# Two accumulator banks for probabilities times values, and a ring of two banks for the other steps

## The reference

```
x = LN(x + attention0(x))      # 16 query heads on 4 key/value heads, RMS norm, rotary, full softmax
x = LN(x + experts(x))         # top 1 of 8 experts, gate/up/down of width 512, and a shared expert of the same width
x = LN(x + attention1(x))      # 16 heads of 16, biases, causal softmax
x = LN(x + mlp(x))             # 256 -> 1024 -> 256, relu, 4 bit weights with scales, low-rank additions
attention:  probs = softmax(q k^T / 4);  out = (probs v) Wo
```

## Time and profile before

| | |
|---|---|
| median of 3 runs | 843.1 us (842.71 to 844.33) |
| the profiled execution's own time | 843.22 us |
| its span in the profile | 841.4 us |
| TensorE busy | 773.6 us (92%) |
| VectorE busy | 449.0 us (53%) |
| ScalarE busy | 357.3 us (42%) |
| mean granted TensorE clock | 0.982 |
| first layer's attention | 35 to 248 us |
| tiles of the experts | 286 to 422 us |
| second layer's attention | 498 to 788 us |

### The profile page before, as it was taken

The page is one execution under the profiler, slowest core; times in us unless marked ns, Lnnn a source line. Parts: engine busy times, 40 slices in busy tenths (PEclk is TensorE's granted clock), DMA queues, the critical chain, the costliest instruction groups (busy, mean ns, idle before and its releaser), DMA issues. The chain is left out here.

```text
span 841.4 us, 11574 instructions
## 1 busy us (share of the span) xinstructions
PE 773.6 (92%) x3933; PEld 410.9 (49%) x3934; DVE 449.0 (53%) x1202; ACT 357.3 (42%) x561; POOL 115.7 (14%) x127
## 2 busy tenths in 40 slices
PE   7899999999999999999997979888998999889886
PEld 3323435444335466666664444344464445433675
DVE  4662852563446522222266767868655775672453
ACT  3498785784872112212134233445413532246030
POOL 0000000000000311112851501131001100022000
PEclk9999999999999999999999999989999999999999
DMA  6767026006026251111137850017200460000000
GB/s 220 202 212 263 1 80 183 1 30 184 0 79 222 66 165 48 44 44 44 32 91 226 239 149 1 1 35 234 60 1 2 133 194 1 2 1 26 14 13 25
DMA packets 52029, 75.01 MB, mean 89 GB/s; under 512 B 7670, under 2 KB 44826, under 8 KB 50058
## 3 DMA queue, kind: packets, MB, share of 16 engines
q1 hardware_dynamic: 50108, 69.26, 27.2%
q0 software_dynamic: 1872, 5.11, 2.3%
HBM read 46.57 MB, written 27.66 MB: 88 GB/s over the span
## 5 line engine op out<-in xcount | busy, mean ns | idle before, releaser
L659 PE MATMUL ps<-arena 128*128 128x256 f32 (+3 forms) x1084 | 323.1, 446 | 18.1 <-ACT arena L1066 3.0
L659 PEld LDWEIGHTS ps<-arena 128*128 128x128 f32 x1084 | 199.0, 193 | 104.7 <-issue 66.2
L992 ACT ACTIVATE arena<-ps 128x1024 f32<-128x1024 f32 x128 | 124.0, 1030 | 26.2 <-PE ps L727 25.7
L1089 ACT ACTIVATE arena<-ps 128x1024 f32<-128x1024 f32 (+3 forms) x128 | 82.9, 702 | 114.3 <-PE ps L919 114.2
L1475 DVE TENSOR_REDUCE arena<-ps 128x1 f32<-128x512 f32 (+3 forms) x176 | 100.5, 634 | 27.6 <-PE ps L897 26.7
L785 PE MATMUL ps<-arena 128*128 x184 | 86.5, 593 | 0.6 <-DVE arena L1199 0.6
L1590 POOL TENSOR_SCALAR_AFFINE_SELECT arena<-arena 128x512 f32<-128x512 f32 x64 | 41.9, 655 | 254.1 <-ACT arena L1089 254.1
L727 PE MATMUL ps<-arena 96*128 96x512 bf16 x256 | 69.8, 382 | 4.4 <-ACT arena L992 3.0
L895 PE MATMUL ps<-arena 96*128 96x128 bf16 (+3 forms) x256 | 62.6, 304 | 9.6 <-DVE arena L1475 5.4
L741 PE MATMUL ps<-arena 128*32 128x512 f32 x512 | 68.8, 604 | 0.2 <-ACT arena L999 0.2
L1020 ACT ACTIVATE arena<-ps 128x512 f32<-128x512 f32 x23 | 13.8, 598 | 108.5 <-PE ps L785 108.5
(11 more groups left out here) (160 smaller groups left out, 700.5 us busy)
## 6 DMA issues: line engine op xcount, KB each, us to landing
arena<-stacks_dram SPq DMA_DIRECT2D x16, 768.0 KB, 6.3
arena<-in_gate_up_proj SPq DMA_DIRECT2D x8, 1024.0 KB, 9.3
stacks_dram<-arena SPq DMA_DIRECT2D x16, 384.0 KB, 3.3
arena<-in_down_proj SPq DMA_DIRECT2D x8, 512.0 KB, 9.0
stacks_dram<-arena SPq DMA_DIRECT2D x16, 256.0 KB, 3.5
q_stacks_dram<-arena SPq DMA_DIRECT2D x8, 384.0 KB, 3.2
arena<-q_stacks_dram SPq DMA_DIRECT2D x8, 384.0 KB, 4.7
arena<-q_stacks_dram SPq DMA_DIRECT2D x4, 768.0 KB, 6.1
```

What stands on the lines that cost most here:

```text
L659: last = nc.tensor.matmul(dst[0:rows, lo:hi], a, w, start=(n == 0), stop=(n == len(pairs) - 1))
L992: nc.scalar.activation(probs[:, 2 * p:2 * p + 2, :], ps[:, 2 * p:2 * p + 2, :], ACT.Exp)\
L1089: nc.scalar.activation(cprobs[:, i % 2, 2 * p:2 * p + 2, P * kt:S], ps[:, 2 * p:2 * p + 2, P * kt:S], ACT.Exp).then_inc(exp_done[p], 1)
```

## The change

UNITS goes from 3 to 2, so the ring has banks 6 and 7. Bank 5 becomes a second accumulator: group hg of four heads uses bank 4 + hg % 2, for writing and for reading, in both layers. The first P of a group now waits for the evacuation of the group before the last. The order of the steps, their instructions and everything else stay.

```diff
--- before.py
+++ after.py
@@ -49,7 +49,7 @@
 BLOCK = 64
 HG = NH // 4
 STACK = 6 * HD
-UNITS = 3
+UNITS = 2
 WIDE = 4
 OPENING = ("max", 0)
 LN_EPS = 1e-5
@@ -733,12 +733,12 @@
                     hg, kt = i // NT, i % NT
                     if i == 0:
                         pe.wait_ge(v_ready, b + 1)
-                    if kt == 0 and HG * b + hg >= 1:
-                        pe.wait_ge(o_evac, HG * b + hg)
+                    if kt == 0 and HG * b + hg >= 2:
+                        pe.wait_ge(o_evac, HG * b + hg - 1)
                     for g in range(4):
                         if g % 2 == 0:
                             pe.wait_ge(exp_done[g // 2], k + 1)
-                        last = nc.tensor.matmul(ps[32 * g:32 * g + 32, 4, :], v_aug[:, kt, hg, :],
+                        last = nc.tensor.matmul(ps[32 * g:32 * g + 32, 4 + hg % 2, :], v_aug[:, kt, hg, :],
                                                 (probs0, probs1)[i % 2][:, g, :], start=(kt == 0), stop=(kt == NT - 1))
                     last.then_inc(pv_done, 1)
                 elif n == "P":
@@ -926,10 +926,10 @@
                         consumed(pe, ("cV", b, 0))
                         consumed(pe, ("cV", b, 1))
                     if kt == 0:
-                        pe.wait_ge(o_evac, HG * (B + b) + hg)
+                        pe.wait_ge(o_evac, HG * (B + b) + hg - 1)
                     pe.wait_ge(masked, headc * b + i + 1)
                     for g in range(4):
-                        last = nc.tensor.matmul(ps[32 * g:32 * g + 32, 4, P * kt:S],
+                        last = nc.tensor.matmul(ps[32 * g:32 * g + 32, 4 + hg % 2, P * kt:S],
                                                 cv_aug[:, b % 2, kt, 4 * hg + g, :],
                                                 cprobs[:, i % 2, g, P * kt:S], start=(kt == 0), stop=(kt == NT - 1))
                     last.then_inc(pv_done, 1)
@@ -996,7 +996,7 @@
                     if b and i == NT - 1:
 
                         act.wait_ge(at_ready, 2 * b)
-                    nc.scalar.activation(o_sb[:, i // NT, :], ps[:, 4, :], copy).then_inc(o_evac, 1)
+                    nc.scalar.activation(o_sb[:, i // NT, :], ps[:, 4 + i // NT % 2, :], copy).then_inc(o_evac, 1)
                 elif n in ("X", "N"):
                     dst = {"X": x_t, "N": x1_of[b]}[n]
                     src = filled(act, step).rearrange("p (t c n) -> p t c n", t=2, c=2)
@@ -1483,7 +1483,7 @@
                     nc.vector.tensor_tensor(mparts[:, :, 1, :], mneg, mparts[:, :, 0, :], ALU.subtract).then_inc(m_parts, 1)
                 elif n == "cF":
                     v.wait_ge(pv_done, head0 * B + headc * b + NT * (i + 1))
-                    nc.vector.transpose(co_sb[:, i, :], ps[:, 4, :]).then_inc(o_evac, 1)
+                    nc.vector.transpose(co_sb[:, i, :], ps[:, 4 + i % 2, :]).then_inc(o_evac, 1)
                     v.wait_ge(o_evac, HG * (B + b) + i + 1)
                     rows_of(i, co_sb[:, i, :], c_a_t, cattn, rden, cat_ready, 2 * b)
                 elif n == "cP":
```

## The result

The changed kernel takes 890.8 us (median of 4 runs, 887.28 to 896.16), the one before 843.7 in the same comparison. The ratio is 1.0555 with a 95% interval of 1.0493 to 1.0618, so the change costs 47 us (42 to 52 by the interval). The profiled execution took 891.1 us with a span of 889.3.

A forecast was written before the change was run, and what follows sets the result against it. TensorE, busy 773.6 of 841.4 us and taking steps in fixed order, was taken as the bound. Terms of 42.7 us less 0.4 gave 42.3, cut by a tenth to 38: 843 + 38 = 881 us, range 860 to 895.

The forecast's parts named there:

- part 1: Accumulator banks in both layers: at most 2.6 us of waits removed, 2.2 worth nothing at the value projections, 0.4 us gained.
- Row maxima: Layer 1's attention in the later three batches: each of 37 runs of maxima costs one reduction, 0.60 us, 22.2 in all.
- The single places: Places in both layers and the tail where a bank's consumer is late, each worked from when step u-2's bank comes free.
- gate: Shared gate of batch 0: the third fill waits 4.3 us for ScalarE's silu, less 0.64 standing today: 3.7 us.
- down step: Down projection of batch 2: second D waits 4.3 us for VectorE's add, less 0.78 the next step waits today: 3.6.
- tail: Up steps at the end: the first waits, the second follows one fill (0.9 us) later, 0.3 for one more: 1.2 us.
- rival 2: Clock falls to 1.2 GHz for a third of the maxima stretches: at most 41 us on top of 38; 900 us; chance 0.08.
- short packs: Nine places of short fills (start projections, normalised rows, layer 1's first weights), 0.3 to 1.4 us each, estimated at 5.0 us.
- The allowance: Whole kernel: a tenth off the 42.3 us sum, for waits that do not move with TensorE, leaving 38.
- Rival 1: Whole kernel: the waits are mostly swallowed in TensorE's idle time, 10 to 20 us lost, 853 to 863 us; chance 0.15.
- Rival 3: Row maxima: two banks are enough as VectorE sets the pace; only the accumulator counts, 2.6 us gained, 840.5 us; chance 0.04.

The follow-up runs named there:

- second profile: The changed kernel, unchanged, profiled a second time: 887.3 us; the kernel before, also profiled again: 845.1 us.
- filling the wait: Changed kernel plus matmuls on constants during the waits before batch 2's second down step and the last batch's first up step: 887.5 us against 890.7 unfilled.

## Why the prediction was right, and where it was off

It forecast 881 us in a range of 860 to 895, slower with 0.96; the kernel takes 890.8. The loss is 47 us with an interval of 42 to 52: the 38 forecast are below it, the plain sum of 42.3 is at its lower edge. The method held: compare the start of every step with the emptying of the step two before it, and add up along the engine that takes its steps in order.

- *The accumulators give 0.4 us* (part 1): right as far as can be told. Their waits are gone, and taking the second one back changes nothing that can be measured; the 1.1 us stand at cV instead.
- *Row maxima, 22.2 us*: 20.7 measured, and alone on two banks 19.5. The size was right, but "one reduction for each of 37 runs" was right in part by luck. The list has 13, 13 and 12 runs; the forecast left out the four of the first stretch between transposes of weights and counted 14 in each of the others. In the first stretch 5.4 was forecast and 4.6 measured, in the later two 16.8 and 16.1. But part of that is waiting for the emptied projection, up to 1 us is the lower clock at the ends, and with reductions shorter by 40% the loss fell only from 20.7 to 17.9 us.
- *The single places*: gate 3.69 us of wait (3.7 forecast net of 0.64; a smaller wait of 0.39 for the same silu stands before it), down step 4.32 less the 0.78 (3.6 forecast), tail 3.71 less 1.71. The forecast put the tail at 1.2, one fill more, which makes it 0.8 too small.
- *The term that is missing* is the clock behind the new waits, which the sum puts at nothing and only rival 2 names. Layer 0 was put at 12.6 us with its short packs (3.7 + 2.3 + 3.6 and about 3 of the 5.0). The changed kernel loses 19.8 until the first expert matmul, 15.9 in its second profile; the 4 us between the two arise before 45 us. 1.7 us of it is the clock behind the down step, shown by filling the wait. Of the gate, the drawn-out matmuls at clock 0.57 are seen (2.79 for 1.88, 1.87 for 1.07: 1.7 us), but that wait wasn't filled.
- *The allowance*, "I take a tenth of the whole off", is 4.2 us, spread over everything. The lag of the same matmuls behind the kernel before shows where it belongs (times of the kernel before; the packs are split as about 3 and 2 us):

| | forecast, without the allowance | lag added | in the second profile |
|---|---|---|---|
| up to the experts | 12.6 | 19.7 | 15.9 |
| from there to 508 us | 3.9 | 1.0 | 0.9 |
| from 508 us to the end | 25.8 | 27.2 | 27.3 |
| in all | 42.3 | 47.9 | 44.1 |

Between the experts and 508 us the lag rises from 19.7 to 27.9 and falls back to 20.7: nearly all that is added there is swallowed. In the other two parts nothing speaks for an allowance. What is missing there is about the clock behind the three long waits, 1.7 + 1.7 + 1.6 = 5.0 us, and in the first profile the 4 us of the start. All in all the changed kernel has 21 us more at the lower level (11 in the second pair of profiles). At that level TensorE does half the work, so this is worth up to 11 us (6), an estimate; how it splits over the other places stays open.
- *Rival 1* (swallowed) holds at one place: around 452 us, where a removed wait comes back. *Rival 2* (the clock): its sign, a clock below 1.00 in the maxima, came true for the last 4 us of the later two stretches (0.51 and 0.53 in the 7 us from there), and its size did not: about 1 us in each, where it gave 20 us or more in all. Most of the lower level stands elsewhere, some of it behind the few long waits. *Rival 3* was refuted by putting only the maxima on two banks.

The Trainium skill ("TensorE: Matmul & The Clock Gate", A second HAM failure mode: psum-queue depth-cycling) tells of a kernel whose clock swung from small idles between groups of matmuls. The trace agrees at two places: the clock fell at 667 and 769 us, behind waits of at most 0.43 us. In the 49 us ahead of each, with waits of the same kind up to 1.2 us long, it stayed at 1.00.

## What to carry to other kernels

On an engine with a fixed order, a bank that serves many steps can be worth far more than one that removes a few waits: compare, for each step of the ring, its start with the emptying of the step that would now share its bank, and add the differences along that engine. Take off only where the next waits are on a chain that does not move: here that was one stretch, between the experts and the second attention. Before a wait is booked as a gain, look at the step behind it, which may stand for the same consumer anyway. And a long new wait can cost more than its length: here the matmuls behind waits of 3.7 to 4.3 us ran at the lower clock. So the clock deserves a term of its own.

## What was not expected of the hardware

Behind single waits of 3.69, 4.32 and 3.71 us the granted clock was 0.57, 0.69 and 0.66 over the next 4 to 5 us, and the matmuls took 1.6 to 1.7 us longer than behind a filled wait, in both places tried. But a long wait is not what sets the clock alone. Behind two waits for the same late copies of query projections, 2.43 us at 603 and 2.40 us at 704, the clock was 1.00 once and 0.57 the other time, and the same eight matmuls took 1.99 and 3.56 us. In two runs a projection behind the same wait of 0.8 us ran at 1.00 and at 0.66. And it fell in the maxima behind waits of at most 0.43 us, at the same two places in both profiles. What decides between such cases is not shown here.
